# Four decay totals and the product of the keys with beta on GpSimd in place of VectorE

## The reference

```python
q = _causal_dwconv_silu(_l2norm(x @ Wq), conv_q); k = _causal_dwconv_silu(_l2norm(x @ Wk), conv_k)
v = _causal_dwconv_silu(x @ Wv, conv_v)
beta = sigmoid(x @ Wb)
g = -exp(A_log) * softplus((x @ Wfa) @ Wfb + dt_bias)
# for each token, with a state of 128 x 128 per head:
S = S * exp(g)[:, None]
err = v - k @ S
S = S + beta * k[:, None] * err[None, :]
o = (q * D ** -0.5) @ S
# then an RMS norm of o, a sigmoid gate, and the product with Wo
```

## Time and profile before

| what | value |
|---|---|
| time, median of 3 runs | 865.34 us |
| runs | 861.22, 865.34, 868.65 us |
| profiled execution, own time | 863.03 us |
| its span, first to last instruction | 861.0 us |
| mean granted TensorE clock | 0.980 |
| TensorE busy | 790.3 us |
| VectorE busy | 754.5 us |
| ScalarE busy | 680.9 us |
| GpSimd busy | 164.6 us |

### The profile page before, as it was taken

The page is one execution under the profiler, slowest core; times in us unless marked ns, Lnnn a source line. Parts: engine busy times, 40 slices in busy tenths (PEclk is TensorE's granted clock), DMA queues, the critical chain, the costliest instruction groups (busy, mean ns, idle before and its releaser), DMA issues.

```text
span 861.0 us, 44394 instructions
## 1 busy us (share of the span) xinstructions
PE 790.3 (92%) x20010; PEld 545.7 (63%) x20010; DVE 754.5 (88%) x1553; ACT 680.9 (79%) x1780; POOL 164.6 (19%) x274
## 2 busy tenths in 40 slices
PE   3888669999999999999999999999999998898976
PEld 3634235667666766676766767667666666777764
DVE  6736589999999999899999999999999999878644
ACT  3255567999989989899899989999999899667741
POOL 8000011221211122121222211112222222111210
PEclk9999878999999999999999999999999999999999
DMA  6311222221100123111112222111111111000002
GB/s 152 98 37 37 71 66 62 62 62 41 41 21 25 61 62 98 61 41 41 41 41 61 62 64 85 51 41 41 41 39 36 37 29 38 16 16 5 4 2 49
DMA packets 33936, 41.68 MB, mean 48 GB/s; under 512 B 5266, under 2 KB 25044, under 8 KB 33748
## 3 DMA queue, kind: packets, MB, share of 16 engines
q1 hardware_dynamic: 33748, 38.85, 15.6%
HBM read 37.60 MB, written 1.25 MB: 45 GB/s over the span
## 4 chain that ended last, share of the span: by engine, by line
PE 70%; DVE 17%; ACT 8%; DMA 2%; issue 2%; SPq 0%; DVEq 0%
PE psum L941 17%; PE psum L1089 6%; PE psum L976 5%; DVE qkv L1407 5%; PE psum L1003 4%; PE psum L1021 4%; PE psum L1054 3%; PE psum L1067 3%; PE psum L1061 3%; PE psum L1040 3%; PE psum L951 3%; PE psum L947 2%; PE psum L1047 2%; PE psum L957 2%; PE psum L1073 2%
## 5 line engine op out<-in xcount | busy, mean ns | idle before, releaser
L1407 DVE SCALAR_TENSOR_TENSOR qkv<-pad,chan,qkv 128x512 f32<-128x512 f32 x288 | 215.3, 791 | 12.0 <-ACT qkv L659 9.3
L941 PE MATMUL psum<-hT,gw 128*128 128x512 f32 x384 | 196.8, 639 | 6.7 <-DVE pad L1404 5.4
L1457 DVE TENSOR_TENSOR kq<-kq,tot 128x512 f32<-128x512 f32 x160 | 120.5, 768 | 0.0
L941 PEld LDWEIGHTS psum<-hT,gw 128*128 128x128 f32 x384 | 68.8, 198 | 68.3 <-issue 64.2
L1472 DVE COPY_PREDICATED pairs<-masks,psum 128x256 f32<-128x256 uint8 x160 | 86.6, 544 | 7.1 <-PE psum L976 6.5
L506 POOL TENSOR_TENSOR inverse<-turned,corner 128x256 f32<-128x256 f32 x32 | 34.7, 1083 | 287.4 <-DVE turned L1424 287.4
L635 ACT ACT_TABLE_LOAD x58 | 74.4, 1283 | 3.9 <-DVE qkv L1407 2.8
L664 ACT ACTIVATE sdec<-state,gamma 128x128 f32<-128x128 f32 x232 | 70.9, 390 | 0.0
L1463 DVE TENSOR_TENSOR ks<-ks,tot 128x256 f32<-128x256 f32 x160 | 66.0, 412 | 5.1 <-PE psum L976 5.0
L1003 PE MATMUL psum<-natural,pairs 32*32 32x16 f32 x4096 | 61.3, 181 | 3.8 <-issue 2.0
L1089 PE MATMUL psum<-gwo,oT 128*128 128x256 f32 x256 | 63.6, 393 | 0.9 <-ACT oT L700 0.9
(11 more groups left out here) (178 smaller groups left out, 1743.5 us busy)
## 6 DMA issues: line engine op xcount, KB each, us to landing
rr<-norm_rows SPq DMA_DIRECT2D x32, 512.0 KB, 3.7
bb<-beta_rows SPq DMA_DIRECT2D x32, 256.0 KB, 4.4
gw<-in_L_attn_Wq SPq DMA_DIRECT2D x16, 128.0 KB, 2.4
gw<-in_L_attn_Wk SPq DMA_DIRECT2D x16, 128.0 KB, 2.5
gw<-in_L_attn_Wv SPq DMA_DIRECT2D x16, 128.0 KB, 2.3
gwo<-in_L_attn_Wo SPq DMA_DIRECT2D x4, 512.0 KB, 5.2
x<-in_L_attn_hidden_states SPq DMA_DIRECT2D x4, 256.0 KB, 4.8
gfb<-in_L_attn_Wfb SPq DMA_DIRECT2D x16, 64.0 KB, 2.7
```

What stands on the lines that cost most here:

```text
L941: last = eng.matmul(two(bank[to]), gw[:, t, kt, hh * D:(hh + 1) * D], two(hT[:, kt])[:, :, h * PW:(h + 1) * PW], start=(kt == 0), stop=(kt ...
L1407: return eng.scalar_tensor_tensor(out=piece(t, i), in0=pad[:, t, :, tap:tap + PW], scalar=tap_weight(t, tap, i), in1=piece(t, i), op0=ALU. ...
L1457: return eng.tensor_tensor(right, right, lower.rearrange("p (a n o) -> p a n o", a=1, o=1).broadcast_to((P, 2, HU // h, h)), ALU.mult)
```

## The change

The four totals that VectorE computed (64, 32, 16 elements and gamma) and the product of the keys with beta become instructions of GpSimd, with the same shapes and operands. `next_totals` and `beta_landed` move to GpSimd's block. GpSimd's slot gets a new order: the fourth total and the key product of the next chunk come first, then the history, then the fifth total between history out and the power, then gamma, then the block placement, and last the first three totals of the chunk after the next (they stood at the start of the following slot before). Semaphores `totals3_ready` and `totals4_ready` are new, `gamma_ready` is gone. Some waits change with it.

```diff
 # GpSimd's slot
+                n8 = t - 8
                 if 0 <= n9 < NCK:
-                    after(dec_ready, n9 + 4)
-                    if n9 <= 1:
-                        after(queries_decayed1, n9)
-                    block_totals(q, 0, chunk(dec, n9 % NCH)).then_inc(totals1_ready, 1)
-                    after(totals1_ready, n9 + 1)
-                    block_totals(q, 1).then_inc(totals2_ready, 1)
+                    after(totals3_ready, n9 + 1)
+                    next_totals(q, 3).then_inc(totals4_ready, 1)
+                    after(kraw_ready, n9 + 1)
+                    beta_landed(n9 + 1)
+                    after(kst_done, n9 - 1)
+                    eng.tensor_tensor(ks[:, q], kraw[:, 0], bb[:, q], ALU.mult).then_inc(kb_ready, 1)
                 if 0 <= i5 < NCK:
                     after(q_tap3, i5)
                     history_in_of(i5).then_inc(history_in, 1)
...
                     eng.tensor_copy(hist[:, i5 % G], pad[:, :, :, PW:]).then_inc(history_out, 1)
+                if 0 <= n9 < NCK:
+                    if n9 >= 28:
+                        after(totals4_ready, n9 + 1)
+                    next_totals(q, 4).then_inc(totals5_ready, 1)
                 if 0 <= n11 < NCK:
                     after(rms_sum, n11 + 1)
                     eng.tensor_tensor(ssq[:, 2], ssq[:, 1], mhalf[:, :], ALU.pow).then_inc(rms_ready, 1)
+                if 0 <= n9 < NCK:
+                    after(totals5_ready, n9 + 1)
+                    after(sdec_ready, n9 - 1)
+                    next_totals(q, 5)
                 if 0 <= n10 < NCK:
                     after(turned4_ready, n10 + 1)
                     place_blocks(p).then_inc(blocks_placed, 1)
+                if 0 <= n8 < NCK:
+                    after(dec_ready, n8 + 4)
+                    if n8 <= 1:
+                        after(queries_decayed1, n8)
+                    block_totals(p, 0, chunk(dec, n8 % NCH)).then_inc(totals1_ready, 1)
+                    after(totals1_ready, n8 + 1)
+                    block_totals(p, 1).then_inc(totals2_ready, 1)
+                    after(totals2_ready, n8 + 1)
+                    next_totals(p, 2).then_inc(totals3_ready, 1)
 # ScalarE's slot
                 if 0 <= n2 < NCK:
-                    if n2 >= 31:
-                        after(gamma_ready, n2 + 1)
                     decay_state(p, n2).then_inc(sdec_ready, 1)
...
-                    if im5 <= 3:
+                    if im5 <= 5:
                         after(history_out, im5)
 # TensorE's slot
-                    if im5 <= 4:
+                    if im5 <= 5:
                         after(k_normed, im5)
 # VectorE's slot
-                    if im5 <= 3:
-                        after(history_out, im5)
+                    after(history_out, im5)
                     after(k_tap3, im5)
                     normalize(1, im5).then_inc(k_normed, 1)
                     after(q_tap3, im5)
                     normalize(0, im5).then_inc(q_normed, 1)
-                if 0 <= n1 < NCK:
-                    next_totals(q, 5).then_inc(gamma_ready, 1)
-                if 0 <= nm1 < NCK:
-                    after(kraw_ready, nm1 + 1)
-                    beta_landed(nm1 + 1)
-                    after(kst_done, nm1 - 1)
-                    eng.tensor_tensor(ks[:, q], kraw[:, 0], bb[:, q], ALU.mult).then_inc(kb_ready, 1)
...
                     decay_even(q, chunk(dec, nm1 % NCH))
+                    after(totals1_ready, nm1 + 1)
                     decay_odd(q)
...
-                if 0 <= nm1 < NCK:
-                    next_totals(q, 3)
-                if 0 <= n0 < NCK:
-                    next_totals(p, 4).then_inc(totals5_ready, 1)
...
                 if 0 <= n0 < NCK:
-                    after(totals5_ready, n0 + 1)
                     decay_queries(p, 5).then_inc(queries_decayed5, 1)
...
-                if 0 <= nm2 < NCK:
-                    after(totals2_ready, nm2 + 1)
-                    next_totals(p, 2)
```

More of the change, by code:

```diff
@@ L200, in build @@
             "diag_done diag_ready ks_even level0_done kept0 totals2_ready")
[L201 to L220, removed]
@@ L221, in build @@
-        x_added, = sems(
-            "x_added")
+        level1_done, kept1, queries_decayed1, level2_done, queries_decayed2, totals3_ready = sems(
+            "level1_done kept1 queries_decayed1 level2_done queries_decayed2 totals3_ready")
+        level3_done, kept3, queries_decayed3, totals4_ready, kept4, queries_decayed4 = sems(
+            "level3_done kept3 queries_decayed3 totals4_ready kept4 queries_decayed4")
+        totals5_ready, level5_done, kept5a, kept5b, queries_decayed5, keys_decayed5 = sems(
+            "totals5_ready level5_done kept5a kept5b queries_decayed5 keys_decayed5")
@@ new lines, in build @@
+        natural0_ready, y1_done, y1_ready, natural1_done, natural1_ready, turned1_ready = sems(
+            "natural0_ready y1_done y1_ready natural1_done natural1_ready turned1_ready")
+        y2_done, y2_ready, natural2_done, natural2_ready, turned2_ready, y3_done = sems(
+            "y2_done y2_ready natural2_done natural2_ready turned2_ready y3_done")
+        y3_ready, natural3_done, natural3_ready, y4_done, y4_ready, natural4_done = sems(
+            "y3_ready natural3_done natural3_ready y4_done y4_ready natural4_done")
@@ new lines, in build @@
+        natural4_ready, turned4_ready, blocks_placed, y5_done, y5_ready, turned5_done = sems(
+            "natural4_ready turned4_ready blocks_placed y5_done y5_ready turned5_done")
+        r_done, rs_ready, u_done, us_ready, kst_done, kst_ready = sems(
+            "r_done rs_ready u_done us_ready kst_done kst_ready")
+        sdec_ready, s_done, state_ready, o_done, osq_ready, gate_done = sems(
+            "sdec_ready s_done state_ready o_done osq_ready gate_done")
+        og_ready, rms_sum, rms_ready, on_ready, ot_done, ot_ready = sems(
+            "og_ready rms_sum rms_ready on_ready ot_done ot_ready")
@@ L223, in build @@
+        wo_done, x_added = sems(
+            "wo_done x_added")
         block = ctx.enter_context(nc.Block())
@@ L501, in block_totals, with next_totals @@
                 return eng.tensor_tensor(tots[1][:, 0].rearrange("p (m n) -> p m n", m=G * B), lower, upper, ALU.mult)
+            def next_totals(p, l):
+                lower, upper = totals(p, l)
+                return eng.tensor_tensor(tots[l + 1][:, p] if l < NL - 1 else gamma[:, p], lower, upper, ALU.mult)
             def place_blocks(p):
@@ L511, in history_in_of, with beta_landed @@
                 return eng.memset(pad[:, :, :, 0:TAPS - 1], 0.0)
+            def beta_landed(count):
+                if count > 0:
+                    eng.wait_ge(in_beta[(count - 1) % 2], 16 * ((count - 1) // 2) + 16)
             def early_inverse():
@@ L1463, in decay_keys @@
                 return eng.tensor_tensor(half(ks[:, p], h, 0), half(ks[:, p], h, 0), spread(upper, h), ALU.mult)
-            def next_totals(p, l):
-                lower, upper = totals(p, l)
-                return eng.tensor_tensor(tots[l + 1][:, p] if l < NL - 1 else gamma[:, p], lower, upper, ALU.mult)
             def keep_pairs(p, l):
@@ L1477, in landed @@
                     eng.wait_ge(sem, 16 * min(count, NCK))
-            def beta_landed(count):
-                if count > 0:
-                    eng.wait_ge(in_beta[(count - 1) % 2], 16 * ((count - 1) // 2) + 16)
             def slot(t):
@@ L1485, in slot @@
                 im5 = t + 5
-                nm2 = t + 2
                 nm1 = t + 1
```

## The result

The changed kernel takes 869.52 us (median of 17 runs, 864.3 to 873.98) where the kernel before takes 862.71 (17 runs, 856.35 to 868.65): a ratio of 1.0072, interval 1.005 to 1.0094. Run again beside 30 runs of the kernel before it gave 1.0059 [1.0035, 1.0082], so the loss of 5 to 6 us repeats, and the forecast of 864.3 us (859 to 869) missed it. The kernel before, run again against itself, gave 1.0012 [0.9983, 1.004]. Ratios and mean clocks here leave out the few executions that took over 1.5% longer than the fastest of the same kernel.

What follows compares the result with a forecast made beforehand. The prediction took TensorE, without a gap in periods of 22.38 us, as the bound. Its terms (0, -0.7, -1.2, 0, +0.6, +0.3) summed to -1.0 us from the shown median of 865.34, giving 864.3 us, range 859 to 869.

Steps and rivals of the forecast that it cites:

- Full periods 0: Main loop's full periods: TensorE has no gap and keeps its 22.37 to 22.38 us, so 0 change.
- The three waits -0.7: Full periods where VectorE also scales output weights: TensorE's three waits for the output sum vanish, -0.7 us.
- The end of the full part, -1.2: 716 to 740 us: VectorE's relief shortens TensorE's 1.7 us of waits, -1.2 us (bounds 0 and -1.7).
- Contention: Full periods: GpSimd's product beside VectorE's PSUM-reading normalizations costs VectorE 0.1 us (bounds 0 and 0.8).
- rival A: Full periods: GpSimd blocks VectorE, which becomes the bound; +0.65 us in each of 24 periods, +15.6, 880 us; 7%.
- Start +0.6: Loop start: the first product ends later on GpSimd, beside two decays with two SBUF inputs; +0.6 us.
- next period +0.3: Second period: the product falls beside taps and decays on the path to normalized keys; +0.3 us (0 to +0.6).
- Draining periods: Loop's end: GpSimd's product ends at the moment when TensorE reaches the diagonal products; 0 us (0 to +0.5).
- B: Loop periods: GpSimd's product comes late, needing over 2.4 us; at 3.0 us +14, 879 us; 3%.
- C: Odd periods of up to 24.6 us: shorter VectorE work takes back their 6.7 us too; up to -8, 857 us; 10%.

Runs made afterwards that it cites:

- middle_early_beta: Changed kernel with the key product on GpSimd only for chunks 2 to 26 and the last three beta rows loaded early; 0.9968 of the kernel before.
- drain_on_vector: Changed kernel with the key product of the last five chunks back on VectorE; 1.0007 of the kernel before.
- totals_early_beta: Changed kernel with the key product back on VectorE and the last three beta rows loaded early; 1.0018 of the kernel before.
- totals_only: Changed kernel with the key product back on VectorE, only the four totals staying on GpSimd; 0.9982 of the kernel before.

## Why the prediction was wrong

- **Full periods 0: right.** 22.37 us with TensorE full, and 25 products on GpSimd there cost nothing that can be told (middle_early_beta, drain_on_vector). VectorE waits for the diagonal products before the key decay, as forecast (8.0 us in 24 periods). The product took 1.28 us instead of 1.1, inside its bounds, from 0.17 us after the key turn in the last full periods.
- **The three waits -0.7: right.** They are gone from the trace. The end of the full part, -1.2, is right by TensorE's waits: of 0.51 and 0.79 us for the key decay (chunks 27 and 28) and 0.4 for the state only 0.53 us, in chunk 28, are left. It doesn't show in the time, for the same stretch holds the 1.99 us stop.
- **Contention: right place, wrong reach.** I argued that the product lies beside PSUM readers and costs VectorE about 0.1 us; beside the normalizations nothing is seen (676 ns). I knew the mechanism, as rival A for the full periods, and even priced it in the start, where two decays lie beside the product, but never asked what stands behind the product when the normalizations have run out.
- **Start +0.6 and next period +0.3: right in sum.** TensorE waits 0.65 us more for the first product, and about 1 us is lost over the profiles, though all of it by the turn of chunk 0.
- **Draining periods "0 (0 to +0.5)": the step that failed, in two parts.** Its reason, that the product ends at the moment when TensorE reaches it, was true of the diagonal products and looked no further. The path from there goes through VectorE's two decays to the key decay, and the first of these got 0.1 us of work done beside the product: TensorE stands 0.36 to 0.37 us later in each of chunks 29 to 31, 1.1 us together. With that figure in place of 0 the sum would be +0.1 instead of -1.0, still far from the measured 5 to 6 us.
- **No term for TensorE's stops and its clock in the drain.** This is the larger part. The mean clock is 0.9728 against 0.9789 over the runs; in work at full clock that is 0.0061 x 870 = 5.3 us at the most. Over all kernels, each against the kernel before of the same series, the clock is 0.0025 to 0.0061 lower with the drain's products on GpSimd, and between 0.0021 lower and 0.0024 higher with them on VectorE. How much time goes with it is less clear: within the runs of one kernel the time falls by 5 to 11 us for 0.01 of clock, but in the changed kernel's own two series by 6.0 (without the execution at 0.936) and 2.6, which makes anything from 1.6 us to all of the loss. A longer stop lengthens a run and is followed by a lower clock, so the two aren't separate causes. The table puts both into the drain. That the product in the last five chunks brings the time is shown (1.0046 with it alone, 1.0007 without it). By which link it brings longer stops isn't: the beta rows may have a share (clock 0.9769 when they are early), but totals_early_beta stopped for 2.76 us without any, and a wait of 0.39 us for the key decay stands in chunk 30 of totals_only too, whose ratio is 0.9982. That stays open.
- **Rivals.** A, B and C did not come. A had the right mechanism at the wrong place: its 15.6 us asked for contention in 24 periods, and the part of the loss that is traced to contention came from three. The loss of 0.6 to 0.7% is within the 1% that I held for the least that can be told; the 17 runs of each kernel told it. The forecast stood on a median of 865.34 from three runs, which 17 runs put at 862.71; so where the sum had -1.0, the measured difference of the medians is +6.8, a miss of nearly 8 us and not of the 5.2 between 864.3 and 869.5. That the high base hid part of the miss is chance.

## What to carry to other kernels

Read a moved instruction's neighbours on the other engines in every stage, above all where the loop drains: what covers it in a full period (here two PSUM readers) is often the first work to run out. A VectorE instruction with two SBUF inputs that starts behind a long GpSimd one should be priced as ending its own time after that one, less about 0.1 us, and a GpSimd one that starts second as delayed in turn. And where the bound engine idles in a stage already, don't write 0 for it without runs: look at its stops and at the granted clock behind them, execution by execution, for there they cost more than the waits that could be worked out.

## What the runs showed of the hardware

- A GpSimd product of 512 elements blocks a VectorE instruction with two SBUF inputs almost wholly (0.65 to 1.59 us when it starts 0.24 us behind, 1.34 when 0.48 behind; in both it ends 0.56 us after the product), while it costs one that reads PSUM and one SBUF tile nothing (676 ns). The product takes 1.27 us in both cases; where it started 0.24 us behind a VectorE decay with two SBUF inputs it took 1.57 us, and 1.80 where they started together.
- TensorE stopped for 2.0 and 2.2 us in the drain with no engine to wait for, and went on 1.2 and 1.4 us after a 16 KB instruction packet had landed. Both packets had started as a 256 KB row was ending, but a stop of 2.76 us in another kernel had no row or other transfer beside it. Half clock followed the first two for 6.8 us each time.
- A kernel's profiled execution can have a granted clock of 0.95 in its full periods, 22.84 us instead of 22.37 for the same 621 matmuls, and a total inside the kernel's usual range (867.78 us of 864.3 to 873.98). No run here shows why.
